# Score products of a language-model block: 128 rows with zeros, or 64 rows in two row groups

## The chip, the core and the metric

The kernel runs on one core of one Trainium2 chip. The metric is device time in microseconds (us) of one execution; lower is better. The engines are TensorE (PE in the profile; its weight loads are PEld), VectorE (DVE), ScalarE (ACT), GpSimd (POOL) and SyncE (SP, which issues DMAs).

## The reference

One layer of a small language model over 2 sequences of 1024 tokens out of a vocabulary of 128, width 512. The token rows h are a normalised and projected table entry. Then an attention of 32 heads over 8 key/value heads of width 16, and a gated FFN of width 2048:

```python
h = _L0_tok_ref(x, ...)                      # emb_table[x], rms_norm, projection, rms_norm
h = h + _L0_attn_ref(_layernorm(h), wq, wk, wv, wo)
h = h + _L0_ffn_ref(_layernorm(h), w_gate, w_up, w_down)
# attention, per head: causal softmax(q k^T / 4) v ;  FFN: down(silu(gate) * up)
```

As h depends on the token alone, so do q, k and v. The kernel scores each token against the 128 vocabulary entries rather than against 1024 positions, takes the exp, and multiplies it by how often each entry has occurred so far (`cT`, the counts). That is the same sum as the causal softmax over positions.

## The kernel before

**Stages.** First tables are built (to 48 us): the token table, the counts, and for each sequence a table of running score maxima, which VectorE scans out of PSUM. The last product there, `score_banks` (line 1001), already multiplies over 64 rows: its left operand lies on partitions 0 to 63 or 64 to 127, and it takes the two row groups in turn, into banks q and q + 4.

Then the 2048 tokens go through in 8 blocks of 256. `phase(n, att, ffn, m)` exists on each engine and walks 24 slots. Phase 0 is the attention of block 0 alone ("the lone attention"). Phases 1 to 7 hold the attention of block n beside the FFN of block n - 1 ("joint"). Phase 8 is the last FFN alone. The order of instructions on each engine is the order in which the code writes them, slot by slot; semaphores are the only other tie.

**One attention unit** V is one key/value head of 128 tokens: four query heads. There are 16 units a block, one in each of slots 0 to 15. In slot s TensorE issues `score(s)`, the transposes `turn(s + 1)` (line 1025, q rows of the next unit), `values` of the unit two or three slots back (lines 1054, or 1060 and 1061), and in joint phases one group of the gate and up products, `gate_up` (24 matmuls of 256 columns, lines 1082 to 1084), in slots 16 to 23 down products instead. In the lone attention filler matmuls (line 1134, numbers in `FILL`) take the place of `gate_up`. Around a unit: ScalarE or VectorE copies q to `Qst` (lines 492, 790), the score product follows (line 1036), ScalarE's exp (517), VectorE's product with the counts (824), in joint phases from block 2 a split into two halves of 16 bits (527, 375), and the value product.

**The score product.** q rows of two heads lie stacked on the partitions, 64 rows each (`STK`). To take one head of the two, the kernel multiplies over all 128 rows with a K tile whose other half is zero: `KstA` holds keys on rows 0 to 63 and zeros below, `KstB` the reverse. So the four heads of a unit are four matmuls of 128 columns into one bank, `b_S[V % 2]`.

**PSUM.** Eight banks: 0 to 2 are `f_bank` (FFN; in the lone attention bank 0 holds the first output tile, bank 1 every other pair of value results, bank 2 the filler and the gram product of the down weights), 3 is q's transposes, 4 and 5 the scores in turn, 6 the value products `b_PV`, 7 `b_tail`. The score of V waits for the exp of V - 2 (`exp_done`, V - 1), which empties its bank. The gram product (line 1140, slots 16 to 19) bounds the down weights; VectorE takes its maximum (745), and the third `gate_up` group of phase 1 waits for it (`dn_max`), since it writes bank 2.

Of the kernel before, what the change touches and what calls it, by code (L numbers as in the profile page):

```python
# [4 lines left out]
ALU = mybir.AluOpType  # L5
ACT = mybir.ActivationFunctionType
AX = mybir.AxisListType
# [64 lines left out]
def lm_block(nc, x_col, embT, emb, nw, projT, wqkv, wo, ffn_w, out, tok_tab, l_tab0, l_tab1, g_tab0, g_tab1):  # L72
    ctx = ExitStack()
    with ctx:
# [22 lines left out]
        KstA = sb("k_stack_even", KV * P, F16)  # L97
        KstB = sb("k_stack_odd", KV * P, F16)
# [91 lines left out]
        b_Q, b_S, b_PV, b_tail = bank16[3], bank[4:6], bank[6], bank[7]  # L190
# [4 lines left out]
        def pv_bank(pair):  # L195
            return f_bank[1] if pair < UPB // 2 and pair % 2 == 1 else b_PV

        def lag(V):
            return 2 if V < WIDE else 3

# [94 lines left out]
        def _(pool):  # L295
# [23 lines left out]
            for kk in (KstA[:, :], KstB[:, :]):  # L319
                last = g.memset(kk, 0.0)  # L320
            last.then_inc(tab["zeroed"], 1)
# [87 lines left out]
        def _(actq):  # L409
# [39 lines left out]
            actq.wait_ge(tab["zeroed"], 4)  # L449
# [17 lines left out]
            a.activation(KstA[0:64, :], bank16[5][0:64, :], ACT.Copy).then_inc(tab["kn_ev"], 1)  # L467
            actq.wait_ge(tab["kn_ev"], 1)
            a.activation(KstB[64:128, :], bank16[5][64:128, :], ACT.Copy).then_inc(tab["kn_ev"], 1)
# [24 lines left out]
            def phase(n, att, ffn, m):  # L494
                at = (FIRST_SLOTS, SECOND_SLOTS, LATER_SLOTS)[min(n, 2)]
                for s in range(SLOTS):
# [13 lines left out]
                    if att and s < UPB:  # L510
                        V = n * UPB + s
                        actq.wait_ge(scores, V + 1)
                        if V >= WIDE + RING:
                            actq.wait_ge(wt_lo, V - RING + 1 - WIDE)
                        elif V >= RING:
                            actq.wait_ge(pv_rdy, V - RING + 1)
                        a.activation(E[V % RING][:, :], b_S[V % 2], ACT.Exp, scale=c_exp).then_inc(exp_done, 1)  # L517
# [59 lines left out]
        def _(dve):  # L577
# [161 lines left out]
            def down_bound():  # L739
                dve.wait_ge(tab["gram"], 1)  # L740
                v.tensor_tensor(t_diag32, f_bank[2][:, 0:P], ident[:, :], ALU.mult).then_inc(tab["dn_diag"], 1)

            def down_max():
                dve.wait_ge(tab["dn_sum"], 1)
                v.tensor_reduce(pm[:, 51:52], f_bank[2][:, P:2 * P], AX.X, ALU.max).then_inc(tab["dn_max"], 1)
# [166 lines left out]
        def _(pe):  # L912
# [98 lines left out]
            pe.wait_ge(tab["kn_ev"], 2)  # L1011
# [16 lines left out]
            def score(V):  # L1028
                gr = V % UPT
                pe.wait_ge(q_st, V + 1)  # L1030
                if V >= 2:
                    pe.wait_ge(exp_done, V - 1)
                r = V % RING
                for j in range(2):
                    for a in range(2):
                        last = t.matmul(b_S[V % 2][:, (2 * j + a) * P:(2 * j + a + 1) * P],  # L1036
                                        (KstA, KstB)[a][:, gr * P:(gr + 1) * P],
                                        Qst[:, r * 256 + j * P:r * 256 + (j + 1) * P], start=True, stop=True)
                last.then_inc(scores, 1)

            def values(V):
                gr = V % UPT
                if V % 2 == 0 and 4 <= V < UPB:
                    pe.wait_ge(pv_ev, V // 2 - 1)
                if V % 2 == 0 and V >= UPB:
                    pe.wait_ge(pv_ev, V // 2)
                r = V % RING
                if V < WIDE:
                    pe.wait_ge(w_rdy, V + 1)
                    if V == 0:  # L1050
                        pe.wait_ge(tab["vf"], 1)
                    for h in range(REP):
                        o = pv_bank(V // 2)[:, ((V % 2) * REP + h) * VFW:((V % 2) * REP + h + 1) * VFW]
                        last = t.matmul(o, E[r][:, h * P:(h + 1) * P], Vf3[:, gr, :], start=True, stop=True)  # L1054
                    last.then_inc(pv_rdy, 1)
                    return
                pe.wait_ge(wt_lo, V + 1 - WIDE)
                for h in range(REP):
                    o = b_PV[:, ((V % 2) * REP + h) * PVW:((V % 2) * REP + h + 1) * PVW]
                    t.matmul(o, WTh[r][:, h * P:(h + 1) * P], Va3[:, gr, :], start=True, stop=False)  # L1060
                    last = t.matmul(o, WTl[r][:, h * P:(h + 1) * P], Va3[:, gr, :], start=False, stop=True)  # L1061
                last.then_inc(pv_rdy, 1)

            def gate_up(m, s):
# [5 lines left out]
                if s == 2 and m == 0:  # L1070
                    pe.wait_ge(tab["dn_max"], 1)
# [15 lines left out]
            def phase(n, att, ffn, m):  # L1087
                at = (FIRST_SLOTS, SECOND_SLOTS, LATER_SLOTS)[min(n, 2)]
                for s in range(SLOTS):
# [39 lines left out]
                    if n == 0 and s == DN_SUM_SLOT:  # L1129
                        pe.wait_ge(tab["dn_diag"], 1)  # L1130
                        t.matmul(f_bank[2][:, P:2 * P], ones32, t_diag32, start=True, stop=True).then_inc(tab["dn_sum"], 1)
                    if n == 0:
                        for _ in range(FILL.get(s, 0)):
                            t.matmul(f_bank[2] if s < min(GRAM) else f_bank[1], id16[:, :], cT[:, 0:512], start=True, stop=True)
                    if n == 0 and s in GRAM:
                        for u in range(*GRAM[s]):
# [3 lines left out]
                            last = t.matmul(f_bank[2][:, 0:P], w, w, start=u == 0, stop=u == 63)  # L1140
# [79 lines left out]
```

## Time and profile before

| | us |
|---|---|
| median of 3 runs | 724.23 |
| lowest, highest | 723.83, 724.27 |
| the profiled execution | 725.0 |
| its span, first to last instruction | 723.3 |
| TensorE busy | 692.8 (96%) |
| VectorE busy | 413.0 (57%) |
| ScalarE busy | 350.1 (48%) |
| GpSimd busy | 294.9 (41%) |

The mean granted clock of TensorE is 0.983 of full speed; it runs at half speed around the end of the table stage and the first units. A matmul's length in the profile is its time in flight: successive ones overlap, so what one costs its engine is the distance from start to start. In a timeline a bracket at the end says how long the engine was idle before the instruction and who released it. "128*128" in a row is the rows and columns of the array that the instruction uses.

### The profile page before, as it was taken

How to read it: one execution, taken by the hardware profiler on the slowest of the kernel's cores; microseconds unless marked ns; L12 is line 12 of the kernel's file. 1: busy time of each engine (PE TensorE's matmuls, PEld its weight loads, DVE VectorE, ACT ScalarE, POOL GpSimd, SP SyncE). 2: the span in 40 equal slices, each digit the busy share in tenths (PEclk: the TensorE clock that was granted, in tenths of full speed). 3: DMA queues.
4: the chain of work that ended last, by engine and by line, in shares of the span. 5: the costliest groups of instructions: out<-in, count | busy, mean ns of one | idle time of the engine just before them, and what ended most of it. 6: DMA issues, size and time to landing. Idle time of an engine off the chain costs nothing.

```text
span 723.3 us, 16202 instructions
## 1 busy us (share of the span) xinstructions
PE 692.8 (96%) x6303; PEld 525.0 (73%) x6303; DVE 413.0 (57%) x1039; ACT 350.1 (48%) x722; POOL 294.9 (41%) x398
## 2 busy tenths in 40 slices
PE   8549989999999999999999999999999999999998
PEld 4328779984898569965997479856996499847873
DVE  6867689886654556554655465554655465543320
ACT  7848378862465226730665146621664066512320
POOL 5020122232366426652465436642665346621220
PEclk9859999999999999999999999999999999999999
DMA  8968310001100120003000110012000300000000
GB/s 325 350 254 314 118 47 1 2 5 56 63 2 1 47 76 1 3 4 103 16 2 2 61 60 2 2 46 76 2 2 1 106 16 2 2 15 15 1 1 29
DMA packets 10458, 40.35 MB, mean 56 GB/s; under 512 B 1808, under 2 KB 2576, under 8 KB 8592
## 3 DMA queue, kind: packets, MB, share of 16 engines
q1 hardware_dynamic: 6912, 25.44, 9.2%
q0 software_dynamic: 3328, 13.11, 5.8%
q8 instruction: 50, 0.82, 0.5%
q10 hardware_dynamic: 144, 0.79, 0.3%
q14 instruction: 24, 0.20, 0.1%
HBM read 29.89 MB, written 9.44 MB: 54 GB/s over the span
## 4 chain that ended last, share of the span: by engine, by line
PE 86%; DVE 7%; ACT 3%; DMA 2%; issue 2%; SPq 0%; POOL 0%; DVEq 0%; ACTq 0%; POOLq 0%
PE banks L1082 15%; PE banks L1084 15%; PE banks L1083 15%; PE banks L1169 6%; PE banks L1171 6%; PE banks L1170 6%; PE banks L1036 4%; PE banks L1054 3%; PE banks L1025 2%; PE banks L1115 2%; PE banks L1117 2%; PE banks L1116 2%; PE banks L1060 1%; PE banks L1061 1%; PE banks L1122 1%
## 5 line engine op out<-in xcount | busy, mean ns | idle before, releaser
L1084 PE MATMUL banks<-xnT_and_h,ffn_weights 128*128 128x256 f16 x1024 | 279.0, 272 | 0.0
L1082 PE MATMUL banks<-xnT_and_h,ffn_weights 128*128 128x256 f16 x1024 | 278.8, 272 | 0.1
L1083 PE MATMUL banks<-xnT_and_h,ffn_weights 128*128 128x256 f16 x1024 | 278.9, 272 | 0.0
L371 POOL TENSOR_TENSOR gated_split<-gate_work,gated_split 128x256 f16<-128x256 f32 x128 | 86.5, 675 | 261.1 <-ACT gated_split L521 261.1
L375 POOL TENSOR_TENSOR weights_split<-weights,weights_split 128x512 f16<-128x512 f32 x96 | 111.0, 1156 | 0.0
L1082 PEld LDWEIGHTS banks<-xnT_and_h,ffn_weights 128*128 128x128 f16 x1024 | 101.0, 99 | 11.9 <-DVE xnT_and_h L874 0.6
L509 ACT ACTIVATE gate_work<-banks,scales 128x256 f32<-128x256 f32 x128 | 60.5, 472 | 100.0 <-PE banks L1084 99.8
L1084 PEld LDWEIGHTS banks<-xnT_and_h,ffn_weights 128*128 128x128 f16 x1024 | 100.0, 98 | 11.7
L1083 PEld LDWEIGHTS banks<-xnT_and_h,ffn_weights 128*128 128x128 f16 x1024 | 99.9, 98 | 11.3
L824 DVE SCALAR_TENSOR_TENSOR weights<-weights,counts_T 128x512 f32<-128x512 f32 x128 | 87.5, 683 | 13.4 <-ACT weights L517 13.3
L517 ACT ACTIVATE weights<-banks,scales 128x512 f32<-128x512 f32 x128 | 87.3, 682 | 14.5 <-PE banks L1036 14.5
L790 DVE COPY q_stack<-banks 128x256 f16<-128x256 f16 x96 | 27.8, 290 | 103.2 <-PE banks L1025 103.2
L812 DVE SCALAR_TENSOR_TENSOR gate_work<-gate_work,banks 128x256 f32<-128x256 f32 x128 | 52.9, 413 | 58.9 <-ACT gate_work L509 58.6
L521 ACT ACTIVATE gated_split<-gate_work 128x256 f16<-128x256 f32 x128 | 53.4, 417 | 67.5 <-DVE gate_work L817 67.5
L1171 PE MATMUL banks<-ffn_weights,gated_split 128*128 128x512 f16 x224 | 84.9, 379 | 0.0
L1170 PE MATMUL banks<-ffn_weights,gated_split 128*128 128x512 f16 x224 | 84.9, 379 | 0.0
L1169 PE MATMUL banks<-ffn_weights,gated_split 128*128 128x512 f16 x224 | 84.9, 379 | 0.0
L527 ACT ACTIVATE weights_split<-weights 128x512 f16<-128x512 f32 x96 | 58.9, 614 | 0.0
L817 DVE SCALAR_TENSOR_TENSOR gate_work<-banks,gate_work 128x256 f32<-128x256 f32 x128 | 54.3, 424 | 4.4
L327 POOL DMA_INDIRECT token_rows<-token_table,indices x16 | 15.7, 981 | 95.4 <-DVE xnT_and_h L860 87.1
L560 ACT ACTIVATE xnT_and_h<-banks 128x512 f16<-128x512 f32 x16 | 9.6, 597 | 80.9 <-PE banks L1122 80.4
L1025 PE MATMUL banks<-ident,token_rows 128*128 128x128 f16 x256 | 35.7, 222 | 9.1 <-DVE token_rows L782 9.1
(230 smaller groups left out, 1083.3 us busy)
## 6 DMA issues: line engine op xcount, KB each, us to landing
ffn_weights<-in_ffn_w SPq DMA_DIRECT2D x12, 1024.0 KB, 11.8
out_rows_dram<-ffn_weights SPq DMA_DIRECT2D x16, 256.0 KB, 2.0
xnT_and_h<-in_wqkv SPq DMA_DIRECT2D x1, 1536.0 KB, 8.3
local_table<-gated_split SPq DMA_DIRECT2D x2, 640.0 KB, 4.7
local_table<-xnT_and_h SPq DMA_DIRECT2D x2, 640.0 KB, 3.6
gated_split<-in_projT SPq DMA_DIRECT2D x4, 256.0 KB, 4.5
ffn_weights<-in_wo SPq DMA_DIRECT2D x1, 1024.0 KB, 10.3
token_table<-weights_split ACTq DMA_DIRECT2D x1, 768.0 KB, 8.3
```

The source lines that it names most:

```text
L371: g.tensor_tensor(gtl[:, j, :], g2[j % 2], gth[:, j, :], ALU.subtract).then_inc(gt_lo, 1)
L375: g.tensor_tensor(WTl[V % RING], E[V % RING][:, :], WTh[V % RING], ALU.subtract).then_inc(wt_lo, 1)
L509: a.activation(th[j % 2], f_bank[j % 3][:, 0:BLK], ACT.Tanh, scale=c_tanh).then_inc(th_rdy, 1)
L517: a.activation(E[V % RING][:, :], b_S[V % 2], ACT.Exp, scale=c_exp).then_inc(exp_done, 1)
L527: a.activation(WTh[V % RING], E[V % RING][:, :], ACT.Copy).then_inc(wt_hi, 1)
L824: v.scalar_tensor_tensor(w, w, SEEN_MAX, cT[:, t * P:(t + 1) * P].unsqueeze(1).broadcast_to([P, REP, P]), ALU.min, ALU.mult).then_inc(w_rd ...
L1082: t.matmul(o, wh, xTh[m % 2][:, c, :], start=c == 0, stop=False)
L1083: t.matmul(o, wh, xTl[m % 2][:, c, :], start=False, stop=False)
L1084: last = t.matmul(o, wl, xTh[m % 2][:, c, :], start=False, stop=c == DC - 1)
L1169: t.matmul(o, hh, dn_w(j, 0), start=j == 0, stop=False)
L1170: t.matmul(o, hh, dn_w(j, 1), start=False, stop=False)
L1171: last = t.matmul(o, hl, dn_w(j, 0), start=False, stop=j == HC - 1)
```

## The change

- The four score matmuls of a unit run over 64 rows: the K tile is one (`Kst`), keys on both halves, and the matmuls alternate between partitions 0 to 63 and 64 to 127. The two row groups write different banks: `score_banks_of(V)` is a pair of banks, 256 columns of each. The exp reads both. The heads then lie in another order in `E`, which `head_block` undoes in the value product.
- The pair is banks 4 and 5. In the lone attention even units take banks 6 and 7 instead. There `score` waits for the exp of V - 2 as before; in the joint phases, with one pair, for the exp of V - 1.
- In the lone attention value results go to banks 1 and 2. The filler of a slot writes bank 4 or 6, and in slots 1 to 15 waits for the exp of the unit before. The gram product and its sum move to bank 6, and the wait for their maximum from `gate_up` to the value product of unit 16.
- `KstA` and `KstB` go, and with them two memsets on GpSimd (line 320) and one of two copies on ScalarE (467, 469).

TensorE, lone attention, slots 1 and 2, before (`banks<-q_stack,k_stack_...` are the scores, `banks<-ident,token_rows` the transposes, `counts_T` the filler, `v_full_one` the values):

```order
L1025 MATMUL banks<-ident,token_rows 128x128 [waits q_stacked,m_ready]
L1025 MATMUL banks<-ident,token_rows 128x128
L1134 MATMUL banks<-counts_T,ident 128x512 x3
L1036 MATMUL banks<-q_stack,k_stack_even 128x128 [waits exp_done,q_stacked]
L1036 MATMUL banks<-q_stack,k_stack_odd 128x128
L1036 MATMUL banks<-q_stack,k_stack_even 128x128
L1036 MATMUL banks<-q_stack,k_stack_odd 128x128
L1025 MATMUL banks<-ident,token_rows 128x128 [waits q_stacked,m_ready]
L1025 MATMUL banks<-ident,token_rows 128x128
```

and after:

```order
L1027 MATMUL banks<-ident,token_rows 128x128 [waits q_stacked,m_ready]
L1027 MATMUL banks<-ident,token_rows 128x128
L1140 MATMUL banks<-counts_T,ident 128x512 [waits exp_done]
L1140 MATMUL banks<-counts_T,ident 128x512 x2
L1039 MATMUL banks<-q_stack,k_stack 128x128 [waits exp_done,q_stacked]
L1039 MATMUL banks<-q_stack,k_stack 128x128 x3
L1027 MATMUL banks<-ident,token_rows 128x128 [waits q_stacked,m_ready]
```

The scores are as many (x3 stands for three alike), the filler has a wait for an exp in front.

TensorE, joint phase 1, the slot of unit 18, before (lines 1082 to 1084 are gate and up; the value product is that of unit 16):

```order
L1084 MATMUL banks<-xnT_and_h,ffn_weights 128x256
L1036 MATMUL banks<-q_stack,k_stack_even 128x128 [waits exp_done,q_stacked]
L1036 MATMUL banks<-q_stack,k_stack_odd 128x128
L1036 MATMUL banks<-q_stack,k_stack_even 128x128
L1036 MATMUL banks<-q_stack,k_stack_odd 128x128
L1025 MATMUL banks<-ident,token_rows 128x128 [waits q_stacked,m_ready]
L1025 MATMUL banks<-ident,token_rows 128x128
L1054 MATMUL banks<-v_full_one,weights 128x17 [waits w_ready,pv_evacuated]
L1054 MATMUL banks<-v_full_one,weights 128x17 x3
L1082 MATMUL banks<-xnT_and_h,ffn_weights 128x256 [waits split_lo,tab_dn_max]
```

and after (1086 to 1088 are gate and up):

```order
L1088 MATMUL banks<-xnT_and_h,ffn_weights 128x256
L1039 MATMUL banks<-q_stack,k_stack 128x128 [waits exp_done,q_stacked]
L1039 MATMUL banks<-q_stack,k_stack 128x128 x3
L1027 MATMUL banks<-ident,token_rows 128x128 [waits q_stacked,m_ready]
L1027 MATMUL banks<-ident,token_rows 128x128
L1059 MATMUL banks<-v_full_one,weights 128x17 [waits w_ready,tab_dn_max,pv_evacuated]
L1059 MATMUL banks<-v_full_one,weights 128x17 x3
L1086 MATMUL banks<-xnT_and_h,ffn_weights 128x256 [waits split_lo]
```

Nothing moves in the order here; the value product has taken over the wait for the gram maximum, and the count behind `exp_done` is one higher.

```diff
@@ -94,8 +94,7 @@
         cT = sb("counts_T", TOK, F16)
-        KstA = sb("k_stack_even", KV * P, F16)
-        KstB = sb("k_stack_odd", KV * P, F16)
+        Kst = sb("k_stack", KV * P, F16)
         Va = sb("v_hi_lo_one", KV * PVW, F16)
@@ -187,16 +186,23 @@
         f_bank = bank[0:3]
-        b_Q, b_S, b_PV, b_tail = bank16[3], bank[4:6], bank[6], bank[7]
+        b_Q, b_PV, b_tail = bank16[3], bank[6], bank[7]
 
...
         def pv_bank(pair):
-            return f_bank[1] if pair < UPB // 2 and pair % 2 == 1 else b_PV
+            return f_bank[2 - pair % 2] if pair < UPB // 2 else b_PV
 
...
             return 2 if V < WIDE else 3
+
+        def head_block(h):
+            return (h % 2) * 2 + h // 2
+
+        def score_banks_of(V):
+            i = 6 if V < UPB and V % 2 == 0 else 4
+            return ps[:, i * 512:(i + 2) * 512].rearrange("p (k x) -> p k x", k=2)[:, :, 0:2 * P]
 
@@ -316,9 +322,6 @@
             g.memset(kst[:, :, MROW:MROW + 2], ONE_K).then_inc(tab["zeroed"], 1)
-            for kk in (KstA[:, :], KstB[:, :]):
-                last = g.memset(kk, 0.0)
-            last.then_inc(tab["zeroed"], 1)
 
@@ -446,7 +449,7 @@
             actq.wait_ge(tab["cols"], 1)
-            actq.wait_ge(tab["zeroed"], 4)
+            actq.wait_ge(tab["zeroed"], 3)
             q3 = bank[7].rearrange("p (h d) -> p h d", d=HD)
@@ -464,9 +467,7 @@
             actq.wait_ge(tab["kn"], 1)
-            a.activation(KstA[0:64, :], bank16[5][0:64, :], ACT.Copy).then_inc(tab["kn_ev"], 1)
-            actq.wait_ge(tab["kn_ev"], 1)
-            a.activation(KstB[64:128, :], bank16[5][64:128, :], ACT.Copy).then_inc(tab["kn_ev"], 1)
+            a.activation(Kst[:, :], bank16[5], ACT.Copy).then_inc(tab["kn_ev"], 1)
             actq.wait_ge(tab["scaled"], 1)
@@ -514,7 +515,8 @@
                             actq.wait_ge(pv_rdy, V - RING + 1)
-                        a.activation(E[V % RING][:, :], b_S[V % 2], ACT.Exp, scale=c_exp).then_inc(exp_done, 1)
+                        a.activation(E[V % RING][:, :].rearrange("p (a x) -> p a x", a=2), score_banks_of(V), ACT.Exp,
+                                     scale=c_exp).then_inc(exp_done, 1)
                     if ffn and 1 <= s <= HC:
@@ -738,11 +740,11 @@
                 dve.wait_ge(tab["gram"], 1)
-                v.tensor_tensor(t_diag32, f_bank[2][:, 0:P], ident[:, :], ALU.mult).then_inc(tab["dn_diag"], 1)
+                v.tensor_tensor(t_diag32, b_PV[:, 0:P], ident[:, :], ALU.mult).then_inc(tab["dn_diag"], 1)
 
...
                 dve.wait_ge(tab["dn_sum"], 1)
-                v.tensor_reduce(pm[:, 51:52], f_bank[2][:, P:2 * P], AX.X, ALU.max).then_inc(tab["dn_max"], 1)
+                v.tensor_reduce(pm[:, 51:52], b_PV[:, P:2 * P], AX.X, ALU.max).then_inc(tab["dn_max"], 1)
 
@@ -1008,7 +1010,7 @@
             score_banks(0, (0, 4))
-            pe.wait_ge(tab["kn_ev"], 2)
+            pe.wait_ge(tab["kn_ev"], 1)
             score_banks(0, (1, 5)).then_inc(tab["s_tab"], 1)
@@ -1029,13 +1031,13 @@
                 if V >= 2:
-                    pe.wait_ge(exp_done, V - 1)
+                    pe.wait_ge(exp_done, V - 1 if V < UPB else V)
                 r = V % RING
...
                     for a in range(2):
-                        last = t.matmul(b_S[V % 2][:, (2 * j + a) * P:(2 * j + a + 1) * P],
-                                        (KstA, KstB)[a][:, gr * P:(gr + 1) * P],
-                                        Qst[:, r * 256 + j * P:r * 256 + (j + 1) * P], start=True, stop=True)
+                        rows = slice(a * STK, (a + 1) * STK)
+                        last = t.matmul(score_banks_of(V)[:, a, j * P:(j + 1) * P], Kst[rows, gr * P:(gr + 1) * P],
+                                        Qst[rows, r * 256 + j * P:r * 256 + (j + 1) * P], start=True, stop=True)
                 last.then_inc(scores, 1)
@@ -1044,6 +1046,8 @@
                     pe.wait_ge(pv_ev, V // 2)
+                if V == UPB:
+                    pe.wait_ge(tab["dn_max"], 1)
                 r = V % RING
@@ -1051,14 +1055,16 @@
                         o = pv_bank(V // 2)[:, ((V % 2) * REP + h) * VFW:((V % 2) * REP + h + 1) * VFW]
-                        last = t.matmul(o, E[r][:, h * P:(h + 1) * P], Vf3[:, gr, :], start=True, stop=True)
+                        e = head_block(h) * P
+                        last = t.matmul(o, E[r][:, e:e + P], Vf3[:, gr, :], start=True, stop=True)
                     last.then_inc(pv_rdy, 1)
...
                     o = b_PV[:, ((V % 2) * REP + h) * PVW:((V % 2) * REP + h + 1) * PVW]
-                    t.matmul(o, WTh[r][:, h * P:(h + 1) * P], Va3[:, gr, :], start=True, stop=False)
-                    last = t.matmul(o, WTl[r][:, h * P:(h + 1) * P], Va3[:, gr, :], start=False, stop=True)
+                    e = head_block(h) * P
+                    t.matmul(o, WTh[r][:, e:e + P], Va3[:, gr, :], start=True, stop=False)
+                    last = t.matmul(o, WTl[r][:, e:e + P], Va3[:, gr, :], start=False, stop=True)
                 last.then_inc(pv_rdy, 1)
@@ -1067,8 +1073,6 @@
                         pe.wait_ge(g2_rdy, i)
-                if s == 2 and m == 0:
-                    pe.wait_ge(tab["dn_max"], 1)
                 if s in (1, 2) and m > 0:
@@ -1128,16 +1132,18 @@
                         pe.wait_ge(tab["dn_diag"], 1)
-                        t.matmul(f_bank[2][:, P:2 * P], ones32, t_diag32, start=True, stop=True).then_inc(tab["dn_sum"], 1)
+                        t.matmul(b_PV[:, P:2 * P], ones32, t_diag32, start=True, stop=True).then_inc(tab["dn_sum"], 1)
                     if n == 0:
+                        if 0 < s < UPB:
+                            pe.wait_ge(exp_done, s)
                         for _ in range(FILL.get(s, 0)):
-                            t.matmul(f_bank[2] if s < min(GRAM) else f_bank[1], id16[:, :], cT[:, 0:512], start=True, stop=True)
+                            t.matmul(bank[4 if s % 2 == 0 else 6] if s < UPB else f_bank[1], id16[:, :], cT[:, 0:512], start=True, stop=True)
                     if n == 0 and s in GRAM:
...
                             w = raw_pair(8 + u // 16).bitcast(BF16)[:, 2 * (u % 16) * P + 1:2 * (u % 16 + 1) * P:2]
-                            last = t.matmul(f_bank[2][:, 0:P], w, w, start=u == 0, stop=u == 63)
+                            last = t.matmul(b_PV[:, 0:P], w, w, start=u == 0, stop=u == 63)
                         if s == max(GRAM):
```

## Rows read from the trace of the kernel before

**Rows 1.** The page: busy time, share and instructions; shares of the chain.
```profile
PE 692.8 (96%) x6303; PEld 525.0 (73%) x6303; DVE 413.0 (57%) x1039; ACT 350.1 (48%) x722; POOL 294.9 (41%) x398
...
PE 86%; DVE 7%; ACT 3%; DMA 2%; issue 2%; SPq 0%; POOL 0%; DVEq 0%; ACTq 0%; POOLq 0%
```

**Rows 2.** Stages: window, length, busy PE PEld DVE ACT POOL, clock, DMA, GB/s.
```profile
64.00:80.00 16.00, 16.00 (x144) 12.67 (x143) 10.54 (x32) 8.27 (x17) 0.00 (x0) 1.00 0.74 270
95.00:175.00 80.00, 78.94 (x696) 65.40 (x696) 68.14 (x125) 56.33 (x117) 19.83 (x27) 1.00 0.04 12
254.00:333.00 79.00, 78.73 (x747) 59.74 (x746) 42.64 (x110) 36.52 (x76) 40.94 (x54) 1.00 0.09 30
```

**Rows 3.** TensorE's waits, 95 to 648 us: total, times, longest (us).
```profile
PE banks L1060 <- ACT pv L542: 1.6, 6, 0.3
PE banks L1036 <- ACT q_stack L492: 1.0, 2, 0.5
```

**Rows 4.** Timeline of a steady slot: start, length (us), instruction, idle before.
```profile
191.08 0.27 PE L1084 MATMUL banks<-xnT_and_h,ffn_weights 128*128 128x256 f16 x1
...
191.19 0.22 PE L1036 MATMUL banks<-q_stack,k_stack_even 128*128 128x128 f16 x1
...
191.36 0.22 PE L1036 MATMUL banks<-q_stack,k_stack_odd 128*128 128x128 f16 x1
...
191.42 0.27 PE L1025 MATMUL banks<-ident,token_rows 128*128 128x128 f16 x2
...
191.76 0.68 ACT L517 ACTIVATE weights<-banks,scales 128x512 f32<-128x512 f32 x1
...
194.15 0.22 PE L1036 MATMUL banks<-q_stack,k_stack_even 128*128 128x128 f16 x1
```

**Rows 5.** Groups by line and shape: busy us, mean ns, idle before.
```profile
L1082 PE MATMUL banks<-xnT_and_h,ffn_weights 128*128 128x256 f16 x1024 | 278.8, 272 | 0.1
...
L1036 PE MATMUL banks<-q_stack,k_stack_even 128*128 128x128 f16 x256 | 42.9, 221 | 1.5 <-ACT q_stack L492 1.0 <-issue 0.5
...
L1001 PE MATMUL banks<-yT_split,gate_work 64*128 64x128 f16 x32 | 1.2, 217 | 1.5 <-DVE yT_split L697 0.9 <-DVE xn L697 0.6
...
L972 PE MATMUL banks<-ident,weights_split 128*128 128x128 f16 x16 | 1.1, 219 | 0.1
```

**Rows 6.** Timeline of the tables' stage; the last row from a window of 0.12 us.
```profile
23.85 1.05 PE L972 MATMUL banks<-ident,weights_split 128*128 128x128 f16 x16
...
28.93 0.62 PE L1001 MATMUL banks<-yT_split,gate_work 64*128 64x128 f16 x16 [0.60 <-DVE xn L697]
...
28.93 0.29 PE L1001 MATMUL banks<-yT_split,gate_work 64*128 64x128 f16 x4 [0.60 <-DVE xn L697]
```

**Rows 7.** Timeline of the lone attention at full clock, units 7 to 9.
```profile
63.13 0.68 ACT L517 ACTIVATE weights<-banks,scales 128x512 f32<-128x512 f32 x1
...
64.17 0.22 PE L1036 MATMUL banks<-q_stack,k_stack_even 128*128 128x128 f16 x1
...
65.37 0.59 PE L1134 MATMUL banks<-counts_T,ident 128*128 128x512 f16 x2
...
65.80 0.22 PE L1036 MATMUL banks<-q_stack,k_stack_even 128*128 128x128 f16 x1
```

**Rows 8.** Timeline of the start of the lone attention.
```profile
48.33 0.38 ACT L492 ACTIVATE q_stack<-banks 128x256 f16<-128x256 f16 x1 [5.78 <-issue]
...
48.85 0.31 PE L1036 MATMUL banks<-q_stack,k_stack_odd 128*128 128x128 f16 x1
...
48.96 0.31 PE L1036 MATMUL banks<-q_stack,k_stack_even 128*128 128x128 f16 x1
```

**Rows 9.** Timeline of the first joint block.
```profile
98.34 0.28 DVE L745 TENSOR_REDUCE part_max<-banks 128x1 f32<-128x128 f32 x1
...
101.83 0.70 ACT L517 ACTIVATE weights<-banks,scales 128x512 f32<-128x512 f32 x1
...
102.53 0.22 PE L1036 MATMUL banks<-q_stack,k_stack_even 128*128 128x128 f16 x1
```


## The prediction

> **What bounds the kernel now.** I read the page first, then the busy time by stage, the groups by line, the waits of TensorE, and last the timelines of three places. The page puts TensorE at 96% of the span and at 86% of the chain that ended last [rows 1]. By stage: from 64 to 80 us (the lone attention) and in the joint blocks it is busy all the time. In a steady block of 79 us VectorE has 42.6 us of work and ScalarE 36.5 [rows 2]. A busy TensorE can hide short idle times, because the ends of matmuls overlap. So I looked at the waits: over the seven blocks with both attention and FFN, 95 to 648 us, TensorE waited 2.6 us in all [rows 3]. What it issues there is the time. An instruction taken from its row there is worth its issue time; a stall added there is lost in full.
>
> The score product of one unit (four heads, 128 tokens) is four matmuls over 128 rows, half of which are zeros. Each shows 221 ns, but that is time in flight. What it costs is the distance of the starts: 191.19 for the first, 191.36 for the fourth, and the next instruction at 191.42: 0.23 us for four, some 0.057 each, in a slot of 2.96 us (191.19 to 194.15) [rows 4].
>
> **The change part by part.**
>
> 1. Scores over 64 rows. The form is in the trace: the tables' stage multiplies over 64 rows, the two row groups in turn, into different banks (line 1001). At full clock 16 of them last 0.62 us with 0.217 us for one: (0.62 - 0.217) / 15 = 0.027 us from start to start, against 16 full-height ones (line 972) in 1.05 us: (1.05 - 0.219) / 15 = 0.055 [rows 5, 6]. So two row groups run side by side, and the rate doubles. The first four of such a run take 0.29 us with the last one's flight, 0.073 of it between the first and the last start [rows 6]. Four scores then occupy 0.11 to 0.13 us in place of 0.22. I take a gain of 0.105 us each. There are 512 score matmuls, 128 units, 16 of them in the lone attention and 112 in the joint blocks, all of which lie in TensorE's unbroken row: 112 x 0.105 = 11.8 us.
>
> 2. The lone attention. Units 7 to 15 follow each other at TensorE's own pace, 1.63 us a slot, with filler matmuls issued in each (64.17 to 65.80) [rows 7]: 9 x 0.105 = 0.95 us. Units 0 to 2 are at the half clock, where starts are 0.11 us apart (48.85, 48.96); TensorE goes on from one unit to the next without a break there, so each gives 0.2: 0.6 us [rows 8]. Around units 3 to 6 ScalarE has squares of weights between the exps, and TensorE comes to wait for its q copies; I count nothing for them. Together 1.55 us.
>
> 3. The wait before the filler, and new banks. In slots 1 to 15 the filler now waits for the exp of the unit before, because it writes that unit's banks. At unit 8 the exp of unit 7 ended at 63.13 + 0.68 = 63.81, and the filler starts at 65.37: 1.6 us of room [rows 7]. What is queued behind this wait is the next score, which needs the same exp. Cost 0. Were the cover gone, the filler and everything behind it would wait for ScalarE. With two bank pairs the score of the lone attention waits for the exp two units back, as before.
>
> 4. One bank pair in the joint blocks. There the score of unit V waits for the exp of V-1, before it was V-2. Queued behind it are the transposes of V+1, the value products and the 24 gate and up matmuls. In the steady blocks the exp ends at 191.76 + 0.68 = 192.44, the next score starts at 194.15: 1.7 us of room [rows 4]. The first joint block is tighter, as ScalarE also splits weights: the exp of unit 17 ends at 101.83 + 0.70 = 102.53, and the score that would wait for it starts at 102.53 [rows 9]. I put one stall of 0.1 us there and none behind it. VectorE is busy for 68.1 of the 80 us of that stage, ScalarE for 56.3 [rows 2], so slots shorter by 0.1 us, under 3%, still fit.
>
> 5. The gram product moves from bank 2 to bank 6. The wait for its maximum moves from the third gate and up group to the value product of unit 16. That maximum is taken at 98.34 + 0.28 = 98.62 us, 3.9 us before even the score of unit 18 [rows 9]: 0.
>
> 6. One K tile. ScalarE copies it once over 128 rows, instead of twice in turn over 64 (about 1.0 us less), and GpSimd clears 2.3 us less. ScalarE sits idle for 5.78 us before the first q copy [rows 8]: 0. The exp reads two banks of 256 columns rather than one of 512. No row shows such an exp; it writes the same 512 elements as the one of 0.68 us, and 0.1 us more would vanish in the 1.7 us of step 4.
>
> 7. The price that no row shows: changing between 128 and 64 rows. In the tables' stage every change of height has a wait in front of it. In the change each unit's scores lie between full-height matmuls, so there are two changes per unit, 224 in the joint blocks. From below the price is 0: the steps between forms that do show are seamless: from the last up product (256 columns, 191.08) to the first score (128 columns) 0.11 us, from the last score to the transposes 0.06 [rows 4]. From above it is a full drain: the next matmul starts only when the last is out. An up product is in flight for 272 ns and its successor starts 110 ns after it, a score 221 and 57: 162 ns on the way in and 164 ns on the way out [rows 4, 5], 0.33 us per unit, three times the gain. Between ends this far apart I go by the nearest row, the unbroken starts across forms, and take 0; both ends stay in the range.
>
> The Trainium skill speaks against that value: "TensorEngine Tiling (Array Packing)", Key Properties, says that a change of tiling mode, not merely of tile, drains TensorE. No row here shows such a change without a wait, so the trace neither agrees nor disagrees; by the rule the sum would be the second rival's, by the rows of seamless forms it is the one below.
>
> **Sum.** 11.8 + 1.55 - 0.1 = 13.3 us less. The profiled execution took 725.0 us (span 723.3), so 711.7; the median of the runs, 724.23, is 0.8 lower: 710.9, say 711. If changes cost up to 0.03 us each, 224 x 0.03 = 6.7 us come back: 718.
>
> **The rivals.**
>
> Break-even. If a change of height costs about 0.05 us, two of them eat the 0.105 and nothing is left; the same if the pairs did not run side by side between full-height work. Against the latter stand the halved steps of rows 5. Time: 724.
>
> Slower, by drains. Every unit stalls TensorE twice. Full price: 0.33 - 0.105 = 0.224 us net, x 112 = 25.1, and 9 x 0.224 = 2.0 in the lone attention: 751. With half the price, 0.165 a unit, it is + 0.06 x 121 = 7: 731. It decides from 0.0525 us per change upwards. For it: the flight time (over 160 ns) is long against the column time, so any wait for emptiness costs more than the gain. Against it: no seam of any kind shows in rows 4. The rule named above is this rival's rule.
>
> Late exps. If the score of V waited 0.1 us on exp V-1 in all 14 slots of the first joint block, 1.4 us of the gain would go: 712.3. It changes no sign.
>
> **How the numbers follow.** Forecast with a price of 0 to 0.03: 0.55, 708 to 718 (708 if the side-by-side starts gain 0.115 and units 3 to 6 give theirs too). Between that and no change: 0.03. Break-even: 0.07. Slower by drains: 0.35, 726 to 752, spread evenly, since nothing here tells a full from a half price. A measurement of this kernel tells 0.2% (1.4 us) from nothing. Faster 0.57, same 0.07, slower 0.36. A range that leaves out 2 in 10 runs from 708 to 746.
>
> **What would show it right or wrong.** In the changed profile, in a steady slot: four score starts within 0.09 us and the transposes 0.11 to 0.14 after the first; the distance from the last up matmul to the first score still 0.11; the slot 2.85 us in place of 2.96; the six steady blocks 1.7 us shorter each. TensorE's waits in 95 to 648 us stay under 4 us. Wrong: a distance of more than 0.16 us before the first score or before the first transpose, or score starts still 0.055 apart. Step 4 is wrong if scores wait on the exp line in more than one or two slots.

## The result, and the profile after

The changed kernel takes 739.68 us (median of 4 runs, 736.14 to 755.9); the kernel before, run beside it, 724.25 (4 runs, 723.83 to 727.49). The ratio is 1.0187, 95% interval 1.0133 to 1.024: slower, by some 13.5 us, where 711 was forecast. (The median of four mixes in one disturbed run of 755.9, which the ratio leaves out.) The profiled execution took 740.71 us, its span 738.8, at a mean granted clock of 0.979 against 0.983.

The page after: busy time of each engine, then the head of the chain that ended last.

```profile
PE 707.4 (96%) x6303; PEld 501.7 (68%) x6303; DVE 411.9 (56%) x1039; ACT 349.7 (47%) x721; POOL 292.9 (40%) x396
...
PE 88%; DVE 6%; ACT 2%; DMA 2%; issue 1%; SPq 0%; POOL 0%; DVEq 0%; POOLq 0%; ACTq 0%
```

Against [rows 1], TensorE is busy 14.6 us longer, with the same matmuls; VectorE, ScalarE and GpSimd have no more work than before. So the time went into TensorE's own row.

A steady block of 16 units after, first score to first score:

```profile
core 0: us, PE busy (x) PEld busy (x) DVE busy (x) ACT busy (x) POOL busy (x), PEclk, DMA share, GB/s
272.06:352.24 80.18, 80.01 (x746) 56.59 (x746) 42.62 (x110) 36.51 (x76) 40.93 (x54) 1.00 0.09 29
```

Before, the same block runs from 263.95 to 342.62, 78.67 us: 1.51 us more now, at full clock in both, and the other engines' work in it is as in [rows 2]. "Busy" hides the cause here: 80.01 of 80.18 us count as busy, since matmuls in flight overlap. The starts tell it. TensorE in one steady slot, which answers to [rows 4]:

```profile
194.93 0.29 PE L1039 MATMUL banks<-q_stack,k_stack 64*128 64x128 f16 x4
195.15 0.28 PE L1027 MATMUL banks<-ident,token_rows 128*128 128x128 f16 x2
195.27 0.27 PE L1086 MATMUL banks<-xnT_and_h,ffn_weights 128*128 128x256 f16 x1
...
197.78 0.27 PE L1088 MATMUL banks<-xnT_and_h,ffn_weights 128*128 128x256 f16 x1
197.99 0.28 PE L1039 MATMUL banks<-q_stack,k_stack 64*128 64x128 f16 x4
198.20 0.28 PE L1027 MATMUL banks<-ident,token_rows 128*128 128x128 f16 x2
```

Three distances: from the last up product to the first score 0.21 us (before 0.11); from the first score to the transposes 0.21 (before 0.23); the slot 3.06 (before 2.96). The four scores did run side by side, their lengths of some 0.22 spanning only 0.28 to 0.29 together, as in the tables' stage [rows 6]. Behind them stands a distance that eats up what the side-by-side starts save (0.21 for scores and seam, before 0.23), and in front of them another 0.10 that nothing covers.

The weight loads of the same slot, where the change of form is visible as idle time:

```profile
197.67 0.10 PEld L1088 LDWEIGHTS banks<-xnT_and_h,ffn_weights 128*128 128x128 f16 x1
197.98 0.11 PEld L1039 LDWEIGHTS banks<-q_stack,k_stack 64*128 64x128 f16 x4 [0.21 <-issue]
198.20 0.11 PEld L1027 LDWEIGHTS banks<-ident,token_rows 128*128 128x128 f16 x2
198.27 0.10 PEld L1086 LDWEIGHTS banks<-xnT_and_h,ffn_weights 128*128 128x128 f16 x1
```

The loads of up products start one matmul ahead (197.67, its matmul 197.78). The score's load starts only with its matmul, as does that of the transposes. Over the kernel the waits of the weight loads show the first of the two in one line (columns: total us, times, longest); the gap of some 0.1 us in front of the transposes' load (198.09 to 198.20) is too short for that list:

```profile
PEld banks L1039 <- issue: 30.2, 122, 0.8
```

TensorE's matmul waits from 95 to 660 us, against [rows 3]:

```profile
PE banks L1039 <- ACT weights L518: 1.1, 1, 1.1
PE banks L1066 <- ACT pv L544: 1.0, 6, 0.2
PE banks L1126 <- DVE xn L872: 1.0, 1, 1.0
PE banks L1039 <- ACT q_stack L493: 0.5, 1, 0.5
```

The first is new: one score waited 1.1 us for an exp. The second is the 1.6 us of [rows 3]: once a block the value product waits for its bank, before 0.27 us, now 0.17. The third is not new; before, it stood at 93.1 us, ahead of the window.

**Where the 15.6 us of the span went** (738.83 - 723.26), by the starts of the first scores. Blocks 2 to 7, and the rest of block 1 from unit 18 on: 6 x 1.51 + 1.44 = 10.5. That is 0.10 in each of fifteen slots of a block and nothing behind its last unit, where the shorter wait for the value bank makes up for it. From the first joint score to unit 18: 2.42. Up to the first transposes of the lone attention 2.07, from there to the first joint score 0.66; at the end 0.1 less. Not all of this comes in every execution of the changed kernel: this one shows two stretches at half clock that another (last experiment) does not, one in the tables' stage and this one:

```profile
104.00:107.00 3.00, 3.00 (x17) 2.13 (x15) 2.26 (x4) 2.63 (x7) 0.66 (x1) 0.50 0.01 3
```

### The profile page after: what moved, and what is told of

It reads as the page before. It is cut to its first block, busy times and chain, and to the rows that moved or that the text cites. A ratio compares the mean times of both kernels' runs of the same rounds, so it can differ in the third digit from the quotient of the medians.

```text
span 738.8 us, 16198 instructions
## 1 busy us (share of the span) xinstructions
PE 707.4 (96%) x6303; PEld 501.7 (68%) x6303; DVE 411.9 (56%) x1039; ACT 349.7 (47%) x721; POOL 292.9 (40%) x396
## 4 chain that ended last, share of the span: by engine, by line
PE 88%; DVE 6%; ACT 2%; DMA 2%; issue 1%; SPq 0%; POOL 0%; DVEq 0%; POOLq 0%; ACTq 0%
PE banks L1086 15%; PE banks L1088 15%; PE banks L1087 14%; PE banks L1175 6%; PE banks L1177 6%; PE banks L1176 6%; PE banks L1027 4%; PE banks L1059 4%; PE banks L1039 4%; PE banks L1119 2%; PE banks L1121 2%; PE banks L1120 2%; PE banks L1140 1%; PE banks L1066 1%; PE banks L1067 1%
## 6 DMA issues: line engine op xcount, KB each, us to landing
ffn_weights<-in_wo SPq DMA_DIRECT2D x1, 1024.0 KB, 10.5
```

## Experiments

Each ran beside the kernel before on the same chip; the ratios are to that, with 95% intervals.

**One score of four over 64 rows, in the kernel before.** Same banks, same waits, no side-by-side: only two changes of height per joint unit are added. The rows left out of that matmul are the K tile's zeros.

```diff
+                        rows = slice(STK, 2 * STK) if V >= UPB and j == a == 1 else slice(0, 2 * STK)
                         last = t.matmul(b_S[V % 2][:, (2 * j + a) * P:(2 * j + a + 1) * P],
-                                        (KstA, KstB)[a][:, gr * P:(gr + 1) * P],
-                                        Qst[:, r * 256 + j * P:r * 256 + (j + 1) * P], start=True, stop=True)
+                                        (KstA, KstB)[a][rows, gr * P:(gr + 1) * P],
+                                        Qst[rows, r * 256 + j * P:r * 256 + (j + 1) * P], start=True, stop=True)
```

> The kernel before, with one edit: the fourth score matmul of each joint unit (112 units) runs over rows 64 to 127 instead of all 128, into the same bank as before. So two changes of height per unit, no bank pair, no new wait, nothing side by side. Theory 1 (each change of height costs some 0.10 us, as the distances in the changed kernel say): +0.20 us per unit, +22 us, 746 us; in a steady slot 0.10 us more before the short matmul and 0.10 more before the transposes. Theory 2 (the loss comes with the bank pair, the exp over two banks or the new waits, not with the height): no change, 724. Theory 3 (full drain of the time in flight, 0.16 us a change): +37 us, 761.

Measured 747.96 us against 725.97, ratio 1.031 (1.0284 to 1.0337). TensorE in a steady slot:

```profile
200.60 0.22 PE L1037 MATMUL banks<-q_stack,k_stack_even 128*128 128x128 f16 x1
200.65 0.22 PE L1037 MATMUL banks<-q_stack,k_stack_odd 128*128 128x128 f16 x1
200.71 0.22 PE L1037 MATMUL banks<-q_stack,k_stack_even 128*128 128x128 f16 x1
200.86 0.23 PE L1037 MATMUL banks<-q_stack,k_stack_odd 64*128 64x128 f16 x1
201.02 0.29 PE L1025 MATMUL banks<-ident,token_rows 128*128 128x128 f16 x2
...
203.96 0.22 PE L1037 MATMUL banks<-q_stack,k_stack_even 128*128 128x128 f16 x1
```

Between full-height matmuls the starts are 0.05 to 0.06 apart; in front of the short one 0.15, behind it 0.16. Each change costs 0.10 us. This slot, which holds value products, is 3.365 long, before 3.155; those without value products went from 2.955 to 3.165. So 0.21 a unit, and in the fifteen slots of each block that show it 105 x 0.21 = 22 us, as measured. This is the price that the forecast took as 0.

**Two scores of four over 64 rows, in the kernel before**: the same with `a == 1` in place of `j == a == 1`, four changes a unit.

> The kernel before with the second and the fourth score matmul of each joint unit over rows 64 to 127: four changes of height per unit instead of the two of the one-short-matmul run. Fixed price of 0.10 us per change: +0.40 us per unit, 112 units, +45 us, 771. If the price is paid once per unit (by the first change): as the one-short run, 748.

Measured 772.23 against 725.76 for the kernel before, ratio 1.0631 (1.0601 to 1.0661).

```profile
200.49 0.22 PE L1037 MATMUL banks<-q_stack,k_stack_even 128*128 128x128 f16 x1
200.64 0.23 PE L1037 MATMUL banks<-q_stack,k_stack_odd 64*128 64x128 f16 x1
200.79 0.23 PE L1037 MATMUL banks<-q_stack,k_stack_even 128*128 128x128 f16 x1
200.96 0.23 PE L1037 MATMUL banks<-q_stack,k_stack_odd 64*128 64x128 f16 x1
201.12 0.28 PE L1025 MATMUL banks<-ident,token_rows 128*128 128x128 f16 x2
```

Four starts at 0.15 to 0.17 instead of 0.055; the slot is 3.37 long (no value products in it), 0.42 more, twice the 0.21 of the experiment before. The price is paid at each change.

**The change with 128 rows.** All of the change kept (bank pairs, exp over two banks, filler wait, the wait for the exp of V - 1), but the K tiles with zeros back.

```diff
-                        last = t.matmul(score_banks_of(V)[:, a, j * P:(j + 1) * P], Kst[rows, gr * P:(gr + 1) * P],
-                                        Qst[rows, r * 256 + j * P:r * 256 + (j + 1) * P], start=True, stop=True)
+                        last = t.matmul(score_banks_of(V)[:, a, j * P:(j + 1) * P], (KstA, KstB)[a][:, gr * P:(gr + 1) * P],
+                                        Qst[:, r * 256 + j * P:r * 256 + (j + 1) * P], start=True, stop=True)
```

> The changed kernel with its bank pairs, waits, filler banks and head order, but the score matmuls over 128 rows with the two zero-padded K tiles. Theory 1: the 0.10 us per unit is gone, what is left is one stall at unit 17 (1.1 us) and perhaps a stretch at half clock behind it: 725 to 727. Theory 2: the loss stays, 736 to 740.

Measured 726.79 (12 runs), ratio 1.0013 (0.9998 to 1.0029). In a steady slot:

```profile
187.73 0.27 PE L1093 MATMUL banks<-xnT_and_h,ffn_weights 128*128 128x256 f16 x1
187.84 0.22 PE L1044 MATMUL banks<-q_stack,k_stack_even 128*128 128x128 f16 x1
...
188.06 0.28 PE L1033 MATMUL banks<-ident,token_rows 128*128 128x128 f16 x2
...
190.79 0.22 PE L1044 MATMUL banks<-q_stack,k_stack_even 128*128 128x128 f16 x1
```

0.11 and 0.22 us and a slot of 2.95, as before. So all that the change does beside the height costs at most 0.3%. The steady block takes 78.67 us, as before. What is left is one wait, still there, with which the first joint block (units 16 to 31) takes 87.35 us instead of 86.70:

```profile
PE banks L1044 <- ACT weights L524: 1.1, 1, 1.1
```

**Two matmuls of 256 columns over 64 rows**, one per row group, in place of four of 128. A price that hangs on the weight loads (half as many now) or on the number of matmuls would fall.

```diff
-                for j in range(2):
-                    for a in range(2):
+                for a in range(2):
...
-                        last = t.matmul(score_banks_of(V)[:, a, j * P:(j + 1) * P], Kst[rows, gr * P:(gr + 1) * P],
-                                        Qst[rows, r * 256 + j * P:r * 256 + (j + 1) * P], start=True, stop=True)
+                    last = t.matmul(score_banks_of(V)[:, a, :], Kst[rows, gr * P:(gr + 1) * P],
+                                    Qst[rows, r * 256:(r + 1) * 256], start=True, stop=True)
```

> The changed kernel with two score matmuls of 256 columns per unit instead of four of 128, one per row group. Theory 1 (a fixed price per change of height): the same two changes per unit; two matmuls side by side of 0.107 us take as long as two pairs of 0.055, so equal to the change within 1 us (736 to 740). If the price were in loading weights of the other height (four loads per unit, now two), a unit would gain 0.05 us or more: 5 us less or more, 731 to 735.

Measured 739.04, ratio 1.0178 (1.0153 to 1.0204).

```profile
202.72 0.27 PE L1087 MATMUL banks<-xnT_and_h,ffn_weights 128*128 128x256 f16 x1
202.93 0.28 PE L1038 MATMUL banks<-q_stack,k_stack 64*128 64x256 f16 x2
203.14 0.29 PE L1027 MATMUL banks<-ident,token_rows 128*128 128x128 f16 x2
```

0.21 and 0.21 again, with half as many matmuls and loads: the price is per change.

**Row groups one after the other**: the order upper, upper, lower, lower (the two loops exchanged), meant to take the side-by-side start away.

> The changed kernel with the four score matmuls in the order upper group twice, lower group twice, so that two of the four no longer alternate. If alternation is what lets the groups run side by side, only the middle two overlap: 0.055 us more per unit, +6 us on the change, 743 to 746. If matmuls of different row groups overlap whatever the order, no difference.

Measured 740.01, ratio 1.0189 (1.0158 to 1.022).

```profile
202.93 0.27 PE L1088 MATMUL banks<-xnT_and_h,ffn_weights 128*128 128x256 f16 x1
203.14 0.29 PE L1039 MATMUL banks<-q_stack,k_stack 64*128 64x128 f16 x4
203.36 0.28 PE L1027 MATMUL banks<-ident,token_rows 128*128 128x128 f16 x2
```

Of the two expectations the second came true: the order of the four makes no difference, and they overlap all the same. Windows that cut the x4 row show two of them under way within 0.02 us and the other two 0.07 later, as in the change. Why they start in pairs in this order too is open.

**64 rows in the lone attention alone**: the bank pairs kept, 128 rows in the joint blocks.

```diff
+                        rows = slice(a * STK, (a + 1) * STK) if V < UPB else slice(0, 2 * STK)
```

> The kernel with the bank pairs and 128-row scores, but with 64 rows in the 16 units of the lone attention alone. By 0.10 us more per unit where TensorE sets the pace (13 to 16 units): +1.3 to 1.6 us on the 726.8 of the all-128-row version, 728. If the filler behind the scores covers the change of height there: no difference, 726.8.

Measured 727.82 (12 runs) against 725.76, ratio 1.0023 (1.0006 to 1.0041). TensorE in the lone attention, against [rows 7]:

```profile
65.70 0.59 PE L1146 MATMUL banks<-counts_T,ident 128*128 128x512 f16 x2
66.23 0.23 PE L1045 MATMUL banks<-q_stack,k_stack_even 64*128 64x128 f16 x1
66.23 0.23 PE L1045 MATMUL banks<-q_stack,k_stack_odd 64*128 64x128 f16 x1
66.30 0.22 PE L1045 MATMUL banks<-q_stack,k_stack_even 64*128 64x128 f16 x1
66.30 0.22 PE L1045 MATMUL banks<-q_stack,k_stack_odd 64*128 64x128 f16 x1
...
67.96 0.23 PE L1045 MATMUL banks<-q_stack,k_stack_even 64*128 64x128 f16 x1
```

This is the clearest sight of both effects. Two row groups start at the same hundredth, the pairs 0.07 apart: the gain. From the start of the two fillers to the first score it takes longer than before (65.37 to 65.80 = 0.43, now 65.70 to 66.23 = 0.53), and the slot is 1.73 against 1.63: the price. The ratio of the whole kernel is to the kernel before; against the version with 128 rows throughout it cannot be told from nothing.

**gate_up ahead of the score in phase 1**, in the change: gives the exp of V - 1 the 24 matmuls to finish under, against the new wait of 1.1 us. Two lines: `gate_up(0, s)` for all s moves ahead of `score`.

> The changed kernel with one edit in the first joint block: in each slot the gate and up group is issued ahead of the score, so that between the scores of units 16 and 17 there is a group of 2.6 us and the exp of 16 has time. If the 1.1 us stall of TensorE before the score of unit 17 is lost time: 1.1 us less than the change (by its fastest runs 736.1, so 735.0; median 737 to 739). If it is made up behind: no difference.

Measured 749.34 (6 runs, 738.33 to 756.58), ratio 1.0286 (1.0236 to 1.0336). In the profiled execution, 738.33 us, no score waits for an exp any more from 95 us on, so the wait went as meant. But the runs scatter by 18 us, and the total says nothing on 1 us. In the traces units 16 to 31 take 90.25 us here and 90.56 in the first profile of the change, each with one stretch of 3.4 us at half clock: if anything, 0.3 us are won. Inconclusive; why it scatters is open.

**The same order in the kernel before:**

> The kernel before with the gate and up group ahead of the score in each slot of the first joint block. It waits 0.48 us for a q copy before unit 17; that wait goes: -0.5 us, 723.8 to 725.5 beside 724 to 726 of the kernel before. If the later exps hold up the slots behind, 0 to +1.

Measured 727.71 (12 runs), ratio 1.0016 (0.9999 to 1.0033): no gain.

**Two matmuls of 256 columns over 128 rows, in the kernel before**: the order of heads changed, one matmul for each K tile. Of all versions, the one that might beat both.

```diff
-                for j in range(2):
-                    for a in range(2):
-                        last = t.matmul(b_S[V % 2][:, (2 * j + a) * P:(2 * j + a + 1) * P],
-                                        (KstA, KstB)[a][:, gr * P:(gr + 1) * P],
-                                        Qst[:, r * 256 + j * P:r * 256 + (j + 1) * P], start=True, stop=True)
+                for a in range(2):
+                    last = t.matmul(b_S[V % 2][:, 2 * a * P:(2 * a + 2) * P], (KstA, KstB)[a][:, gr * P:(gr + 1) * P],
+                                    Qst[:, r * 256:(r + 1) * 256], start=True, stop=True)
```

> The kernel before with two score matmuls of 256 columns over 128 rows per unit instead of four of 128 (one per zero-padded K tile, the head order as in the change; one bank, old waits). No change of height at all. Two matmuls issue in 2 x 0.109 = 0.218 us (the gate and up products' distance) beside 4 x 0.056 = 0.225: 0.007 us per unit, -0.9 us over 128 units, 724.9 beside some 725.8. If the narrower form's weight loads cost something that does not show: up to -3 us.

Measured 725.29 (12 runs) against 727.06, ratio 0.9988 (0.9972 to 1.0005). The steady block is 78.59 us against 78.67. The best of those tried, by less than the measurement tells.

**The change once more**, to tell its own cost from that of single executions.

> The changed kernel itself once more, beside the kernel before on the same chip. Steps measured so far: 112 units x 0.10 = 11.2 us in the joint blocks, 1.1 us of stall at unit 17, some 1.5 us in the lone attention: +12 to +14 on the kernel before, 738 to 740; single runs up to 3 us more where a stretch at half clock falls into the tables' stage or behind the stall.

Measured 737.51 (6 runs, 735.45 to 742.12) against 727.06 (17 runs), ratio 1.0163 (1.0134 to 1.0192). The profiled execution has a span of 734.3, 11.0 more than before. It adds up: blocks 2 to 7 6 x 1.51 = 9.1, units 18 to 31 1.44, the first joint score to unit 18 0.75, the lone attention 0.15, start and end -0.4. The steady block:

```profile
267.50:347.68 80.18, 80.01 (x746) 56.52 (x746) 42.63 (x110) 36.51 (x76) 40.94 (x54) 1.00 0.09 29
```

To the hundredth that of the first profile. The wait for the exp is there too:

```profile
100.07 0.29 PE L1039 MATMUL banks<-q_stack,k_stack 64*128 64x128 f16 x4 [1.14 <-ACT weights L518]
```

The remaining 4.5 us of the first profile do not come in every execution: 2.4 lie ahead of the lone attention and 1.7 between units 17 and 18, each with a half-clock stretch that this execution has not, and 0.5 in the lone attention. Whether the change makes the later stretch more frequent is not shown: of the profiles here, three of the seven in which TensorE changes height in the joint blocks have a stretch at half clock after 60 us (the first of the change at 104, two short scores at 105, `gate_up` first at 160), and none of the five others.

## Why the prediction was wrong

**The step that failed is step 7**, "The price that no row shows": between 0 and 0.163 us per change of height I took 0, by "the unbroken starts across forms". Measured: 0.10 us per change, about twice the break-even of 0.0525, and 0.21 a unit. The rows that I went by change columns (256 to 128), not rows; they said nothing of the height. The rival "slower, by drains" had the mechanism and the sign; it put 0.165 a unit for the half price and 0.33 for the full one, and the runs show 0.21. With its own sum the measured price gives (0.21 - 0.105) x 121 = 12.7 us more, 736.9 on the median of 724.23; the two measured ratios give 737.8 and 736.0. So close a match is partly luck: that sum leaves out the new wait (0.66 us), and counts the slots in which the price is made up for. The wide range of 708 to 746 held the time only because it took in this rival. The rule of the Trainium skill that I set aside ("TensorEngine Tiling (Array Packing)", Key Properties: switching the tiling mode drains the engine) agrees in kind with every run here that changes height (0.10 us each). A full drain, as I had worked it out from the lengths in flight, would be 0.16 us; 0.10 is less.

The rows show what the 0.10 consists of. At every change of height amid unbroken work the next matmul starts some 0.07 us before the end that the profile gives for the last one, whatever that one's length: up product to score 197.78 + 0.27 = 198.05 against 197.99, scores to transposes 198.27 against 198.20, filler to score 66.29 against 66.23 (64 rows in the lone attention alone), full to short score 200.71 against 200.64 (two scores of four). Unrounded it is 0.067 to 0.071 at every change without a wait in all these profiles, and at half clock too:

```profile
51.36 2.34 PE L1140 MATMUL banks<-counts_T,ident 128*128 128x512 f16 x5
53.63 0.40 PE L1039 MATMUL banks<-q_stack,k_stack 64*128 64x128 f16 x4
53.96 0.39 PE L1027 MATMUL banks<-ident,token_rows 128*128 128x128 f16 x2
```

(53.70 against 53.63, 54.03 against 53.96.) Between matmuls of one height the next starts far earlier, 0.16 before the end of a score. So a change waits until the last matmul is all but out. The prediction's full drain was the right picture, 0.07 too long at each change: 0.162 - 0.067 = 0.095. The ends are the profile's model; what happens in these last 0.07 us is open.

**Step 1 held in its form.** Side-by-side starts halve the scores' time: 0.07 us from the first to the last start (here as in [rows 6]), and the whole gain of 0.105 is in the net: 0.21 paid, 0.10 left. The gain was real, and twice as much was paid for it.

**Step 2 turned round** by the same price: the lone attention's slots went from 1.63 to 1.73, + 0.1 each in place of - 0.1. At half clock, in units 0 to 2, I expected 0.2 gained. In the profile after, from the fillers to the score of unit 1 it takes 2.27 us (51.36 to 53.63) instead of 2.14, and from the score to the transposes 0.33 instead of 0.42: a loss of 0.04 in all. In front of the scores, then, the change costs 0.14 (unrounded), not the 0.20 of a price that doubles at half the clock. That fits the drain: a filler is in flight for 0.63 there and its successor starts after 0.43, so 0.63 - 0.07 - 0.43 = 0.13 to 0.14.

**Step 3 held**: no filler waited for an exp. **Steps 5 and 6 held**: with 128 rows and all else of the change, the time is that of before within 0.3%, and the exp over two banks takes 683 ns (before 682).

**Step 4 was mis-sized and misplaced.** "One stall of 0.1 us" at unit 18 was one of 1.1 us at unit 17. TensorE and ScalarE there, after:

```profile
101.31 0.29 PE L1039 MATMUL banks<-q_stack,k_stack 64*128 64x128 f16 x4 [0.48 <-ACT q_stack L493]
101.53 0.28 PE L1027 MATMUL banks<-ident,token_rows 128*128 128x128 f16 x2
102.96 0.29 PE L1039 MATMUL banks<-q_stack,k_stack 64*128 64x128 f16 x4 [1.14 <-ACT weights L518]
```

```profile
99.92 0.70 ACT L485 ACTIVATE ffn_weights<-ffn_weights,scales 128x512 f16<-128x512 f32 x1
100.87 0.38 ACT L493 ACTIVATE q_stack<-banks 128x256 f16<-128x256 f16 x1 [0.25 <-PE banks L1027]
101.85 0.38 ACT L493 ACTIVATE q_stack<-banks 128x256 f16<-128x256 f16 x1 [0.60 <-PE banks L1027]
102.13 0.68 ACT L518 ACTIVATE weights<-banks,scales 128x512 f32<-128x512 f32 x1
```

In phase 1 `gate_up(0, 0)` stands ahead of unit 16's score, so between the scores of units 16 and 17 there is nothing but transposes and a value product to cover ScalarE's q copy and exp. I had looked at the first slot that has a `gate_up` between two scores, and not at the one without. With 128 rows the same 1.1 us shows, so it belongs to the single bank pair. Its net cost is less than 1.1, since the kernel before waited 0.47 us for the q copy at the same place: from the score of unit 16 to that of 17 it went from 0.99 us to 1.65, 0.66 more. With 128 rows it is 1.65 as well, so the changes of height cost nothing extra under this wait. "Late exps" came true in one slot instead of fourteen.

## What to carry to other kernels

Splitting a matmul over row groups pays only if more is saved per visit than two changes of height cost, here 0.2 us: four scores of 128 columns save half of that. By these numbers it would take more than some eight of them in a row (an estimate from 0.105 saved by four; no run tried it). Group such work, so that many small-height matmuls follow each other, or leave it at full height with zeros. Where a form never appears beside another without a wait between them, a seamless row of other forms is no evidence: put one such instruction into the kernel, and read the starts.

## What the runs showed of the hardware

- A change between 128 and 64 rows costs 0.10 us at full clock, each way, linear in the number of changes (0.21 a unit for two, 0.42 for four), the same for scores of 128 and of 256 columns, and 0.14 us at the half clock.
- At such a change the next matmul starts 0.067 to 0.071 us before the end that the profile gives for the last one, at either clock and for lengths from 0.22 to 0.63 us. The price is what this leaves: length less 0.07 less the usual distance of starts.
- Busy time does not show it: TensorE counts as busy for 80.01 of 80.18 us in a block that has grown by 1.5 us. The waits of the weight loads do where the gap is long enough: 30.2 us in 122 places, "issue", where before the same line for the scores had 1.6 us in 4 places. With one short score of four it has 1.3 us in 3, though that kernel is 22 us slower: there the distances of the starts alone show it.
- The order of the row groups, alternating or one after the other, made no difference for four matmuls of 128 columns (0.28 to 0.29 us for four either way).
- Single executions of one kernel differ by short stretches at half clock, which come in some and not in others: the two profiles of the changed kernel differ by 4.5 us of span, at a mean granted clock of 0.979 and 0.986. What brings the stretch at 104 us no run here shows. TensorE was at full clock before it and was idle for about half of the 3 us ahead (1.48 of 3.10 us busy from 100.5 to 103.6). The new wait of 1.1 us is not needed for it: the run with two short scores, which has only the waits of 0.5 us for q copies there, shows one too (105.05 to 108.30 us, clock 0.50).
